# A decoder layer on one core: batches, placement and engines of the cross attention's work

## The chip, the cores and the metric

The kernel runs on one core of one Trainium2 chip. The time is the device time of one execution in microseconds (us). Below, "before" is the kernel as it stands, and the engines are TensorE (PE), its weight loads (PEld), VectorE (DVE), ScalarE (ACT), GpSimd (POOL) and SyncE's DMA queue (SP).

## What is computed

One pre-norm decoder layer on x of 2048 rows by 256, all in float32:

```python
x = x + attn(layernorm(x))          # 16 heads of 16, causal, ALiBi bias, softmax, Wo
x = x + xattn(layernorm(x), ctx)    # 16 heads of 64 over 1601 context rows
x = x + ffn(layernorm(x))           # fp8 x fp8 product with scales, bias in bf16

def xattn(query, ctx):              # q = query@Wq+bq, k = ctx@Wk+bk, v = ctx@Wv+bv
    scores = einsum('bqhd,bkhd->bhqk', q, k) / 8
    out = einsum('bhqk,bkhd->bqhd', softmax(scores), v).reshape(1, 2048, 1024)
    out = out @ Wo + bo + query
    return (out - mean(out)) * rsqrt(var(out) + 1e-5) * gamma + beta
```

The change touches the cross attention and the feed-forward part behind it; the self attention stays.

## The kernel before, in words

A Python class, `Order`, writes out by hand one list of stages; every engine's program walks this list in order and emits its own instructions for each stage, with waits on semaphores. So the list's order is each engine's order.

The cross attention goes over 8 head pairs (p = 0 to 7). Rows 0 to 63 of the array belong to a pair's first head, rows 64 to 127 to the second. Queries are cut into four blocks of 512 (b), keys into 13 tiles of 128 (j; the last has 65). A first sweep finds, for each query, the largest score: `pair_chunk` multiplies one tile of 128 queries with a quarter of the keys (400 columns, one bank for each head, L949), and VectorE reduces each bank to a maximum (L1257). There are 64 chunks a pair. `pair_rows` transposes a block's negated maxima on TensorE (L836), and SP's queue carries them into `shifts`. The second sweep makes, for each key tile, the scores of both heads in f32r (`pair_scores`, L964, three products high and low; the first two tiles also add the shifts, L972), ScalarE's exponentials (L1147), and the product with the values in plain f32 (`pair_values`, L984), which adds up in the bank `products`. The exponentials of the tiles are added up by GpSimd (L757, `add`); in pair 7, blocks 2 and 3, by VectorE. `pair_sums` multiplies that sum with ones (L996; in pair 7 the last three tiles go directly, L1002), `pair_invert` takes the inverses on VectorE (L1351), `pair_divide` multiplies (GpSimd L1509; in pair 7, blocks 2 and 3, VectorE L1356), `pair_project` multiplies with Wo (L1015), and VectorE adds the result to the residual (L1366).

There are 11 buffers of exponentials, two for each key tile, so 5.5 tiles. Four banks hold scores (two tiles); three banks go round among the chunks, projections, sums and transposes. Each f32 or f32r matmul leaves one or two records in the trace.

A batch is two key tiles: two stages of scores, then one run of values for the two tiles of the batch before. That makes seven runs for a block's 13 tiles. Everything else stands between these stages by `interleave` and `spread`: the maxima of blocks 2 and 3 of this pair and of blocks 0 and 1 of the next, and the next pair's projections of keys, queries (L782) and values (`value_tiles`, L937), each in a place of its own among the 80 places of a pair. The lags of sums, inverses, division and projection are counted in key tiles, passed in `pair_values`.

Pair 7 starts with `tail_weights`: VectorE quantises the feed-forward weights in one stage (L1220 to L1379). Behind each block's projection stands its `tail`: statistics, second norm, quantisation, transposition, product and store, spread by `TAIL_AT` over key tiles; most is VectorE's, with GpSimd's inverse roots (L1465, L1467).

## Time and profile before

| what | us |
|---|---|
| median of 3 runs | 1875.3 (1869.7 to 1883.9) |
| profiled execution | 1884.2 |
| its span | 1882.4 |
| TensorE busy | 1746.2 (93%) |
| VectorE busy | 1245.9 (66%) |
| GpSimd busy | 988.7 (53%) |
| ScalarE busy | 920.4 (49%) |

The self attention takes the first third of the span, up to about 610 us; the eight pairs of the cross attention follow from 643 us on. Busy times are sums of what the profiler recorded; a busy TensorE can still work below its peak, and the idle time of an engine that does not set the pace costs nothing.

### The profile page before, as it was taken

The page shows a single profiled execution, that of the slowest core. Times are in us where ns is not written, and L with a number is a line of the kernel's source. Part 1 is how long each engine was busy: PE and PEld are TensorE (multiplying, and loading weights), DVE is VectorE, ACT ScalarE, POOL GpSimd, SP SyncE. Part 2 cuts the span into 40 slices and gives each one's busy share as a digit, 9 for nine tenths or more (in the row PEclk, how much of TensorE's full clock was granted, in tenths as well). Part 3 has the DMA queues.
Part 4 walks back from the last instruction along what each step waited for, and adds up shares of the span by engine and source line. Part 5 has one row for each costly group of instructions (what it writes and reads, how often), then busy time and mean ns, then how long its engine had stood idle before and what let it go on. Part 6 is the DMA issues. An engine that isn't in the chain of part 4 may idle for free.

```text
span 1882.4 us, 29743 instructions
## 1 busy us (share of the span) xinstructions
PE 1746.2 (93%) x10698; PEld 886.5 (47%) x10698; DVE 1245.9 (66%) x2465; ACT 920.4 (49%) x1866; POOL 988.7 (53%) x840
## 2 busy tenths in 40 slices
PE   6989999999988999999999999999999999989973
PEld 3544434444444644555555555454555455444431
DVE  5777777778633565665675675666666566576888
ACT  2346666667665244345445444444544544544442
POOL 1000000000001386788898898898899799787311
PEclk9879999989988799999999999999999999989995
DMA  4332303331011000000000000000000000000001
GB/s 117 35 37 36 35 3 37 36 46 56 1 35 56 11 1 1 1 11 4 11 1 4 11 1 4 1 11 4 1 11 4 1 1 4 1 11 12 12 29 39
DMA packets 27947, 34.49 MB, mean 18 GB/s; under 512 B 4299, under 2 KB 25560, under 8 KB 26341
## 3 DMA queue, kind: packets, MB, share of 16 engines
q1 hardware_dynamic: 27354, 30.95, 9.1%
q8 instruction: 87, 1.43, 0.3%
q0 software_dynamic: 448, 1.64, 0.3%
q14 instruction: 58, 0.48, 0.1%
HBM read 14.99 MB, written 4.19 MB: 10 GB/s over the span
## 4 chain that ended last, share of the span: by engine, by line
PE 78%; DVE 16%; issue 3%; ACT 2%; POOL 1%; DMA 0%; ACTq 0%; SPq 0%; DVEq 0%; POOLq 0%
PE psum L984 18%; PE psum L964 14%; PE psum L949 9%; DVE maxima L1257 9%; PE psum L870 8%; PE psum L782 7%; PE psum L820 4%; PE psum L845 4%; PE psum L937 3%; PE psum L1015 3%; PE psum L882 2%; PE psum L996 2%; DVE parts_room L1351 1%; PE psum L897 1%; DVE stats L1204 1%
## 5 line engine op out<-in xcount | busy, mean ns | idle before, releaser
L1257 DVE TENSOR_REDUCE maxima<-psum 128x1 f32<-128x400 f32 (+5 forms) x1664 | 860.2, 580 | 312.0 <-PE psum L949 209.7
L757 POOL TENSOR_TENSOR parts_room<-parts_room,weights_room 128x512 f32<-128x512 f32 (+1 forms) x593 | 741.0, 1285 | 104.3 <-ACT weights_room L1147 104.2
L1147 ACT ACTIVATE weights_room<-psum 128x512 f32<-128x512 f32 (+1 forms) x757 | 406.5, 599 | 475.3 <-PE psum L964 404.9
L1075 ACT ACTIVATE weights_room<-psum 128x512 f32<-128x512 f32 (+3 forms) x640 | 300.1, 534 | 177.8 <-PE psum L845 98.7
L964 PE MATMUL psum<-stack_room,dk_hi 64*128 64x512 f32 (+1 forms) x1408 | 265.0, 410 | 6.5 <-ACT weights_room L1147 3.7
L949 PE MATMUL psum<-k_later,stack_room 64*128 64x400 f32 (+1 forms) x896 | 237.1, 404 | 12.6 <-DVE maxima L1257 11.4
L949 PEld LDWEIGHTS psum<-k_later,stack_room 64*128 64x128 f32 x896 | 128.9, 184 | 202.6 <-issue 124.9
L1471 POOL DMA_DIRECT2D parts_room<-ctx_dram x1 | 1.3, 1281 | 391.0 <-DMA stack_room<-alibi 391.0
L984 PE MATMUL psum<-weights_room,parts_room 128*64 128x512 f32 (+1 forms) x754 | 203.2, 606 | 0.0
L984 PE MATMUL psum<-weights_room,late_room 128*64 128x512 f32 (+1 forms) x760 | 202.3, 604 | 0.0
L845 PE MATMUL psum<-stack_room,stack_room 51*128 51x512 f32 (+3 forms) x640 | 141.0, 440 | 36.1 <-DVE maxima L1257 33.3
L870 PE MATMUL psum<-weights_room,v_self 128*32 128x512 f32 (+3 forms) x1280 | 170.5, 588 | 0.3 <-ACT weights_room L1075 0.3
L964 PE MATMUL psum<-stack_room,dk_lo 64*128 64x512 f32 (+1 forms) x704 | 165.8, 394 | 0.0
L964 PEld LDWEIGHTS psum<-stack_room,dk_hi 64*128 64x128 f32 (+1 forms) x1408 | 139.7, 182 | 43.9 <-issue 18.9
L1465 POOL TENSOR_SCALAR rstd<-meanvar 128x2 f32<-128x2 f32 (+1 forms) x24 | 9.6, 399 | 284.0 <-DVE meanvar L1207 284.0
L820 PE MATMUL psum<-stack_room,stack_room 51*128 51x512 f32 (+3 forms) x640 | 145.1, 457 | 6.0 <-DVE maxima L1257 5.5
L820 PEld LDWEIGHTS psum<-stack_room,stack_room 51*128 51x128 f32 x640 | 64.4, 198 | 130.5 <-issue 120.1
L1351 DVE RECIPROCAL parts_room<-parts_room 128x128 f32<-128x128 f32 x128 | 112.2, 920 | 9.2 <-ACT parts_room L1044 9.2
L845 PEld LDWEIGHTS psum<-stack_room,stack_room 51*128 51x128 f32 x640 | 67.1, 197 | 89.7 <-issue 75.8
L964 PEld LDWEIGHTS psum<-stack_room,dk_lo 64*128 64x128 f32 (+1 forms) x704 | 90.2, 182 | 11.5
L984 PEld LDWEIGHTS psum<-weights_room,late_room 128*64 128x64 f32 (+1 forms) x760 | 50.7, 136 | 83.2 <-issue 81.1
L984 PEld LDWEIGHTS psum<-weights_room,parts_room 128*64 128x64 f32 (+1 forms) x754 | 50.8, 136 | 82.3 <-issue 80.8
(138 smaller groups left out, 1912.3 us busy)
## 6 DMA issues: line engine op xcount, KB each, us to landing
stack_room<-parts_room SPq DMA_DIRECT2D x84, 128.0 KB
x_block<-x_dram SPq DMA_DIRECT2D x8, 512.0 KB, 4.9
x_middle<-x_block SPq DMA_DIRECT2D x4, 512.0 KB, 3.1
x_block<-x_middle SPq DMA_DIRECT2D x4, 512.0 KB, 3.8
out_dram<-x_block SPq DMA_DIRECT2D x8, 256.0 KB, 2.1
stack_room<-parts_room SPq DMA_DIRECT2D x24, 64.0 KB
parts_room<-ctx_dram POOLq DMA_DIRECT2D x1, 1536.0 KB, 7.9
stack_room<-shift_rows SPq DMA_DIRECT2D x64, 2.0 KB
```

The lines of the kernel that those rows point to most:

```text
L757: engine.tensor_tensor(sum_[:kw, :], old[:kw, :], weights[u % NP_WEIGHTS][:kw, :], ALU.add) \
L782: last = engine.matmul(slot[:, 0:n], lhs(kc), rhs(kc), start=kc == 0, stop=kc == DC - 1)
L820: last = engine.matmul(slots[m][:, 0:k1 - k0], q_stack[p % NSTACK][r, i * P:(i + 1) * P], k_stack[p % NSTACK][r, k0:k1], start=True, stop= ...
L845: last = engine.matmul(slots[m][:, 0:n], k_stack[p % NSTACK][r, j * P:(j + 1) * P], q_stack[p % NSTACK][r, q0:q0 + n], start=True, stop=j ...
L870: last = engine.matmul(products[c:c + COL, q0:BQ], v_self[:, j0 + n, h * VW:h * VW + COL], w_self[(s0 + n) % NW][:, m, 0:BQ - q0], start=j ...
L949: filled(use + n, engine.matmul(slot[:, 0:k1 - k0], q_hi[p % 2][r:r + DH2, i * P:(i + 1) * P], k_high(p)[r:r + DH2, k0:k1], start=True, st ...
L964: last = engine.matmul(pair_scores[u % NSCORES][:kw, :], k[r:r + DH2, at:at + kw], q[r:r + DH2, block(b)], start=first and n == 0, stop=no ...
L984: engine.matmul(products[r:r + DH2, :], v_pair[p % 2][:kw, j, r:r + DH2], weights[u % NP_WEIGHTS][:kw, :], start=j == 0, stop=j == NS - 1) \
L1075: engine.activation(w_self[s % NW][:, m, 0:n], bank_of(use + m)[:, 0:n], ACT.Exp, scale=SELF_SCALE).then_inc(emptied(use + m), 1)
L1147: engine.activation(weights[u % NP_WEIGHTS][:kw, :], pair_scores[u % NSCORES][:kw, :], ACT.Exp, scale=CROSS_SCALE).then_inc(pair_exp, 1)
L1257: engine.tensor_reduce(maxima[:, p % 2, i // TB, n, i % TB, ch:ch + 1], bank_of(use + n)[:, 0:real - k0], AX.X, ALU.max) \
L1351: engine.reciprocal(pair_recip[:, cols], pair_recip[:, cols]).then_inc(inverted, 1)
```

## The change

- A block's 13 tiles of scores go in batches of 3, 3, 3 and 4 (`BATCHES`), each followed by one run of values; all but the last run of a block leave their newest tile to the next run (`kept`).
- A second list, `chain`, counts in runs of values: sums follow one run after a block's end, the inverses one and two runs later, the division three, the projection four. In pair 7 the division comes after two runs and the projection after three; in its blocks 2 and 3 after one and two. `pass_step` now stands before each stage of scores.
- `beside` spreads the maxima evenly over the places of a pair except the last run of each block, and puts the next pair's projections directly ahead of given runs (`KEYS_AT`, `QUERIES_AT`, `TILES_AT`), with a keys' projection in the pair's first run. Value tiles of pair 0 stand ahead of the first scores.
- The keys get a third place, `k_spare`, in the room of the x blocks, for pairs 2, 4 and 6; GpSimd clears its last column. The loads of x for the last part wait until it is read.
- The loads of pair p + 2's weights move to the start of pair p.
- The quantisation of the feed-forward weights is cut into five pieces at runs 0, 3, 4 and 7 of pair 7 (`WEIGHTS_AT`).
- In pair 7, blocks 2 and 3, VectorE adds up only the first head's exponentials, GpSimd the second's; VectorE divides only block 3.
- In the tail the row scale is a stage of its own behind the transposition, the addition of beta moves from the statistics to the second norm, and the load of block b + 2 of x stands behind the store of block b; the first two loads stand at pair 7's start.

The diff, cut to its core (removed lines of `build` are left out):

```diff
-SUMS_LAG, PROJECT_LAG, LAST_PROJECT_LAG = 4, TB + 7, TB + 1
+PAIR_ROWS_LAG, FIRST_ROWS_LAG = 2, 1
+INVERT_AT, DIVIDE_AT, PROJECT_AT = (1, 1, 2, 2), 3, 4
+LAST_INVERT_AT, LAST_DIVIDE_AT, LAST_PROJECT_AT = (1, 1, 2, 2), 2, 3
+WEIGHTS_AT = (0, 0, 3, 3, 4, 7)
+BATCHES = (3, 3, 3, NS - 9)
+KEYS_AT, QUERIES_AT, TILES_AT = (0, 3, 3, 4), (7, 7, 8, 11), (11, 12, 15, 15)
+TAIL_AT, TAIL_APART = (1, 4, 7, 10, 13, 13, 15, 17), 3
...
+    def later(self, runs, what):
+        self.chain.append([runs, what])
+    def pass_run(self):
+        for item in list(self.chain):
+            item[0] -= 1
+            if item[0] <= 0:
+                self.chain.remove(item)
+                item[1]()
...
+    def pair_sweep1(self, p, b, lag):
+        steps = [(1, lambda i=i, ch=ch: self.put("pair_chunk", p, i, ch, banks=HP))
+                 for i in range(TB * b, TB * b + TB) for ch in range(len(CROSS_CHUNKS))]
+        steps.append((0, lambda: self.put("pair_negate", p, b)))
+        def rows():
+            self.put("pair_rows", p, b, banks=1)
+        return steps + [(0, (lambda: self.later(lag, rows)) if lag else rows)]
+    def pair_values(self, kept=0):
+        self.pass_run()
+        due, self.pending = self.pending[:len(self.pending) - kept], self.pending[len(self.pending) - kept:]
+        for p, b, j, s in due:
             self.put("pair_values", p, b, j, s)
             if j == NS - 1:
                 self.put("pair_finish", p, b)
                 if p < NP - 1:
-                    self.after(SUMS_LAG, lambda p=p, b=b: self.pair_sums(p, b))
+                    self.later(1, lambda p=p, b=b: self.pair_sums(p, b))
                 else:
                     self.pair_sums(p, b)
-        self.pending = []
     def pair_sums(self, p, b):
         self.put("pair_sums", p, b, banks=1)
-        at_once = 1 if p < NP - 1 else 2 if b < NB - 1 else TB
+        if p < NP - 1:
+            invert, divide, project = INVERT_AT, DIVIDE_AT, PROJECT_AT
+        elif b < NB // 2:
+            invert, divide, project = LAST_INVERT_AT, LAST_DIVIDE_AT, LAST_PROJECT_AT
+        else:
+            invert, divide, project = (1,) * TB, 1, 2
         for t in range(TB):
-            self.after(t // at_once + 1, lambda t=t: self.put("pair_invert", p, b, t))
-        self.after((TB - 1) // at_once + 1 + (at_once < TB), lambda: self.put("pair_divide", p, b))
-        lag = PROJECT_LAG if p < NP - 1 else LAST_PROJECT_LAG if b < NB - 1 else 2
-        self.after(lag, lambda: self.pair_out(p, b))
+            self.later(invert[t], lambda t=t: self.put("pair_invert", p, b, t))
+        self.later(divide, lambda: self.put("pair_divide", p, b))
+        self.later(project, lambda: self.pair_out(p, b))
...
     def pair_sweep2(self, p):
-        batch = []
         def scores(b, j):
+            self.pass_step()
             self.put("pair_scores", p, b, j, self.step)
-            batch.append((p, b, j, self.step))
+            self.pending.append((p, b, j, self.step))
             self.step += 1
-        def values():
-            self.pair_values()
-            self.pending, batch[:] = list(batch), []
         steps = []
         for b in range(NB):
-            for j0 in range(0, NS, 2):
-                steps += [(1, lambda b=b, j=j: scores(b, j), b) for j in range(j0, min(NS, j0 + 2))]
-                steps.append((min(NS, j0 + 2) - j0, values, b))
+            j0 = 0
+            for n in BATCHES:
+                steps += [("scores", lambda b=b, j=j: scores(b, j)) for j in range(j0, j0 + n)]
+                j0 += n
+                steps.append(("values", lambda kept=int(j0 < NS): self.pair_values(kept)))
         return steps
...
     def tail(self, b):
-        self.put("tail_load", b)
         banks = {"turn": 1, "product": 1}
-        for n, kind in enumerate(("statistics", "add_norm", "to_fp8", "rounded", "turn", "product", "store")):
+        def store(i):
+            self.put("tail_store", b, i)
+            if i and b + 2 < NB:
+                self.put("tail_load", b + 2)
+        for n, kind in enumerate(("statistics", "add_norm", "to_fp8", "rounded", "turn", "row_scale", "product")):
             for i in range(2):
                 self.after(TAIL_AT[n] + TAIL_APART * i,
                            lambda kind=kind, i=i: self.put("tail_" + kind, b, i, banks=banks.get(kind, 0)))
+        for i in range(2):
+            self.after(TAIL_AT[-1] + TAIL_APART * i, lambda i=i: store(i))
...
+    def key_block(self, p, b):
+        self.put("project_keys", p, b, banks=1)
+        self.put("key_steps", p, b)
+        if b:
+            self.put("key_rests", p, b - 1)
+    def query_block(self, p, b):
+        self.put("project_queries", p, b, banks=1)
+        if b == 0:
+            self.put("key_rests", p, NK - 1)
+    def tile_block(self, p, n):
+        self.put("value_tiles", p, n, banks=1)
...
+    def beside(self, main, maxima, others):
+        runs = [n for n, (kind, _) in enumerate(main) if kind == "values"]
+        places = [n for n in range(len(main)) if n not in runs[len(BATCHES) - 1::len(BATCHES)]]
+        ahead = [[] for _ in main]
+        for block, steps in enumerate(maxima):
+            groups = []
+            for work, step in steps:
+                if work:
+                    groups.append([])
+                groups[-1].append(step)
+            here = places[len(places) * block // len(maxima):len(places) * (block + 1) // len(maxima)]
+            for n, group in enumerate(groups):
+                ahead[here[n * len(here) // len(groups)]] += group
+        for n, step in others:
+            ahead[runs[n]].append(step)
+        for (_, step), side in zip(main, ahead):
+            for what in side + [step]:
+                what()
...
+        now(self.pair_queries(0) + self.pair_sweep1(0, 0, 0))
+        def block(make, p, n):
+            return lambda: make(p, n)
+        for n in range(len(VALUE_TILES)):
+            self.tile_block(0, n)
         for p in range(NP):
+            maxima = [self.pair_sweep1(p, b, FIRST_ROWS_LAG if (p, b) == (0, 1) else PAIR_ROWS_LAG)
+                      for b in range(NB // 2 if p else 1, NB)]
+            if p < NP - 1:
+                maxima += [self.pair_sweep1(p + 1, b, PAIR_ROWS_LAG) for b in range(NB // 2)]
+                others = [(at, block(make, p + 1, n)) for make, all_at in
+                          ((self.key_block, KEYS_AT), (self.query_block, QUERIES_AT), (self.tile_block, TILES_AT))
+                          for n, at in enumerate(all_at)]
             else:
+                put("tail_weights_load")
+                put("tail_load", 0), put("tail_load", 1)
+                maxima += [[], []]
+                others = [(at, lambda n=n: put("tail_weights", n)) for n, at in enumerate(WEIGHTS_AT)]
+            if p + 2 < NP:
+                put("pair_load", p + 2)
+            self.beside(self.pair_sweep2(p), maxima, others)
+        while self.chain or self.soon:
+            self.pass_run()
+            self.pass_step()
...
-    def on_vector(p, b):
-        return p == NP - 1 and b >= NB // 2
+    def divided_on_vector(p, b):
+        return p == NP - 1 and b == NB - 1
+    def summed_on_vector(p, b, m):
+        return p == NP - 1 and b >= NB // 2 and m == 0
...
-        return k_later if p else k_first
+        return k_later if p % 2 else k_spare if p else k_first
...
-                    if p >= 2:
-                        act.wait_ge(*bank_filled(use_of["pair_chunk", p - 1, NT - 1, len(CROSS_CHUNKS) - 1] + HP - 1))
+                    if p == 2:
+                        act.wait_ge(normed, 2 * NB)
+                        for i in range(2):
+                            act.wait_ge(middle_out[i], 32)
+                    elif p > 2:
+                        act.wait_ge(*bank_filled(use_of["pair_chunk", p - 2, NT - 1, len(CROSS_CHUNKS) - 1] + HP - 1))
...
-                engine.tensor_tensor(out_scale, scales[:, 0:1], scales[:, 1:2], ALU.mult) \
-                    .then_inc(dve_step, 1)
-                chain.count += 1
-                engine.reciprocal(inv_scales, scales).then_inc(inverse_made, 1)
-                dve.wait_ge(w8_scaled, 1)
+                n, = at
                 flat = w8.rearrange("p c n -> p (c n)")
-                chain.on(quantise(0, flat))
-                after_last()
-                not_a_number_past_448(quant_m[0], flat, quant_m[0])
-                engine.tensor_tensor(flat, flat, quant_m[0], ALU.add).then_inc(w8_made, 1)
+                if n == 0:
+                    dve.wait_ge(tails_in, 16 * 6)
+                    chain.on(engine.tensor_tensor(out_scale, scales[:, 0:1], scales[:, 1:2], ALU.mult))
+                    engine.reciprocal(inv_scales, scales).then_inc(inverse_made, 1)
+                elif n == 2:
+                    dve.wait_ge(w8_scaled, 1)
+                    chain.on(round_unit(0))
+                elif n == 3:
+                    round_up(0)
+                elif n == 4:
+                    chain.on(round_down(0, flat))
+                elif n == 5:
+                    after_last()
+                    not_a_number_past_448(quant_m[0], flat, quant_m[0])
+                    engine.tensor_tensor(flat, flat, quant_m[0], ALU.add).then_inc(w8_made, 1)
             elif kind == "tail_statistics":
                 b, i = at
                 dve.wait_ge(*bank_read(use_of["pair_project", NP - 1, b] + i))
...
+                sp.wait_ge(*bank_filled(use_of["pair_chunk", NP - 2, NT - 1, len(CROSS_CHUNKS) - 1] + HP - 1))
```

## Rows read from the trace of the kernel before

**Rows 1.** The page: the chain that ended last, shares of the span by engine.

```profile
PE 78%; DVE 16%; issue 3%; ACT 2%; POOL 1%; DMA 0%; ACTq 0%; SPq 0%; DVEq 0%; POOLq 0%
```

**Rows 2.** Stretches: us, length, busy us (records) of PE, PEld, DVE, ACT, POOL, then clock, DMA.

```profile
646.75:812.22 165.47, 156.25 (x847) 81.38 (x848) 103.84 (x198) 67.75 (x131) 122.89 (x101) 0.99 0.02 7
812.22:956.32 144.10, 143.54 (x802) 74.51 (x802) 90.92 (x169) 68.86 (x133) 126.56 (x104) 1.00 0.02 5
...
1676.84:1718.02 41.18, 34.23 (x183) 17.80 (x182) 28.31 (x47) 15.10 (x29) 28.32 (x23) 0.88 0.00 1
1718.02:1755.12 37.10, 34.86 (x199) 17.81 (x197) 27.24 (x54) 15.09 (x29) 26.32 (x23) 1.00 0.05 15
1755.12:1790.98 35.86, 33.00 (x178) 15.30 (x177) 31.20 (x70) 18.12 (x37) 5.82 (x9) 0.95 0.07 23
1790.98:1840.90 49.92, 39.49 (x196) 17.17 (x194) 44.01 (x101) 19.07 (x38) 8.74 (x13) 0.93 0.10 31
1840.90:1882.40 41.50, 9.49 (x40) 5.56 (x40) 34.16 (x83) 8.55 (x17) 5.60 (x8) 0.56 0.10 34
```

**Rows 3.** TensorE in time order: start us, duration us, line, output<-inputs, shape, records.

```profile
1125.94 1.94 PE L984 MATMUL psum<-weights_room,late_room 128*64 128x512 f32 x8
1127.80 0.45 PE L949 MATMUL psum<-k_later,stack_room 64*128 64x400 f32 x2
1128.09 0.63 PE L964 MATMUL psum<-stack_room,dk_hi 64*128 64x512 f32 x4
...
1128.79 0.90 PE L949 MATMUL psum<-k_later,stack_room 64*128 64x400 f32 x2
...
1130.59 0.64 PE L984 MATMUL psum<-weights_room,late_room 128*64 128x512 f32 x1
```

**Rows 4.** TensorE in time order: projections and value tiles between f32r work, pairs 2 and 3.

```profile
1041.41 1.98 PE L782 MATMUL psum<-norm_room,parts_room 128*128 128x512 f32 x4
1043.23 1.89 PE L1015 MATMUL psum<-parts_room,parts_room 128*128 128x256 f32 x8
...
1122.88 2.05 PE L937 MATMUL psum<-parts_room,parts_room 128*128 128x128 f32 x16
1124.87 0.73 PE L964 MATMUL psum<-stack_room,dk_hi 64*128 64x512 f32 x4
```

**Rows 5.** All engines in time order, in brackets idle time and its releaser; one batch.

```profile
1002.87 0.18 PEld L949 LDWEIGHTS psum<-k_later,stack_room 64*128 64x128 f32 x2 [0.81 <-issue]
...
1003.35 2.98 DVE L1257 TENSOR_REDUCE maxima<-psum 128x1 f32<-128x400 f32 x6 [1.55 <-PE psum L949]
...
1003.98 0.18 PEld L949 LDWEIGHTS psum<-k_later,stack_room 64*128 64x128 f32 x1 [0.17 <-DVE maxima L1257]
...
1004.05 2.06 ACT L1147 ACTIVATE weights_room<-psum 128x512 f32<-128x512 f32 x4 [5.71 <-PE psum L964]
...
1004.94 0.18 PEld L949 LDWEIGHTS psum<-k_later,stack_room 64*128 64x128 f32 x1 [0.21 <-DVE maxima L1257]
1005.42 0.20 PEld L996 LDWEIGHTS psum<-parts_room,ones_v 128*64 128x64 f32 x4 [0.30 <-DVE maxima L1257]
```

**Rows 6.** GpSimd's additions: count, shortest, median and longest ns of one.

```profile
L757 POOL TENSOR_TENSOR parts_room<-parts_room,weights_room x593: 1255/1283/1705, 656.1 to 1748.9; 128x512 f32<-128x512 f32 x177, 65x512 f32<-65x512 f32 x21
```

**Rows 7.** GpSimd, VectorE, TensorE around pair 7's start; the VectorE line later, alone.

```profile
1678.44 3.10 POOL L757 TENSOR_TENSOR parts_room<-parts_room,weights_room 65x512 f32<-65x512 f32 x2
...
1678.80 1.63 DVE L1224 TENSOR_TENSOR parts_room<-parts_room 128x512 f32<-128x512 f32 x1
...
1685.01 0.70 PE L949 MATMUL psum<-k_later,stack_room 64*128 64x400 f32 x1 [6.91 <-DVE maxima L1257]
...
1807.33 0.69 DVE L1224 TENSOR_TENSOR parts_room<-parts_room 128x512 f32<-128x512 f32 x1
```

**Rows 8.** VectorE's additions after 1738 us (count, busy us, mean ns); TensorE's wait.

```profile
L757 DVE TENSOR_TENSOR parts_room<-parts_room,weights_room 128x512 f32<-128x512 f32 x30 | 18.7, 681 | 0.0
...
1835.54 1.56 PE L996 MATMUL psum<-parts_room,ones_v 128*64 128x512 f32 x4 [4.14 <-DVE parts_room L757]
```

96 lines of the change are left out of this document (34 added, 62 removed).

## The prediction

> **What bounds the kernel now.** I read the views in this order. The chain of waits [rows 1] gives TensorE 78% of the span, VectorE 16%, GpSimd 1%. The stretches [rows 2] say where: I cut them at the first score matmul of head pair 0 (646.75 us), of pair 1 (812.22), of pair 7 (1676.84), at each query block of pair 7, and at the end of its last sums (1840.90). Everything before 646.75 us is untouched except 16 matmuls of value tiles. Pairs 1 to 6, from 812.22 to 1676.84, are one period six times: 864.6 us, 144.1 each; in pair 1, which stands for them, TensorE is busy 143.54 of 144.10, GpSimd 126.56, VectorE 90.92, ScalarE 68.86. So TensorE's queue sets the pace there, GpSimd is 12% behind it. In pair 7 VectorE takes over: busy 31.20 of 35.86 us in block 2 and 44.01 of 49.92 in block 3, and after 1840.90 the last block's chain runs almost alone for 41.50 us.
>
> A busy TensorE is not one at its peak, so I went into the matmuls of one period [rows 3]. Times here are differences of start times. A run of values over two key tiles lasts from 1125.94 to 1127.80: 1.86 us, that is 0.86 a tile (two records of each head side by side, 0.43 a step) and 0.14 on top. Then the kind of matmul changes from f32 to f32r: the first chunk of the maxima costs 0.29 before the score matmul starts, where an undisturbed one costs 0.18. A key tile of scores costs 0.70 (1128.09 to 1128.79), with four products, as for the first two tiles of a block, 0.93. Going back to f32 costs another 0.1. One run of values between f32r work therefore costs about 0.14 + 0.1 + 0.1 = 0.34 us beyond its work. An f32 projection that stands alone before a score tile pays the same; the value-tile block at 1122.88 [rows 4] is one.
>
> The second loss is VectorE's turn on the three banks. In [rows 5] the second matmul of the second chunk loads its weights at 1003.98, 1.11 us after the first chunk at 1002.87, held by VectorE; the next such wait ends at 1004.94, and VectorE needs 2.98 us for six reductions, 0.50 each. The f32 run behind can start 0.48 us after that last load (1005.42). So a burst of chunks is a VectorE-paced chain: the n-th bank is free 1.11 + 0.5 x (n-1) us after the burst began.
>
> **The change, part by part.**
>
> *Batches.* Per query block 7 runs of values become 4 (batches of 3, 3, 3, 4 key tiles; one tile is kept back, so the runs hold 2, 3, 3, 5 tiles). 12 runs fewer per pair x 0.34 = 4.1 us. The 12 projection blocks per pair, of which about 8 stand before a score tile rather than before a run (13 of 20 places of a block are score tiles), now all stand at a run: 8 x 0.3 = 2.4 us. Together 6.5 us.
>
> But the burst gets longer: 4 chunks and 3 tiles. In [rows 3] a batch of two takes 2.79 us from 1127.80 to 1130.59 (the burst of [rows 5] 2.55). For a batch of three, the eighth matmul of chunks waits for the fifth reduction, 1.11 + 4 x 0.5 = 3.11 us; plus 0.48 is 3.58 us. TensorE alone would need 0.29 + 3 x 0.70 + 3 x 0.18 + 0.1 = 3.0, so 0.5 to 0.6 is VectorE's. The batch of four has no chunk before its run: last chunk at about 3.25, then 0.18 + 0.70 + 0.1, so 4.2 us. Block: 3 x 3.58 + 4.2 = 14.9, values 13 x 0.86 + 4 x 0.14 = 11.7, sum 26.7; four blocks 106.7. Around them, as before: sums 4 x 0.91, output projections 4 x 1.83, value tiles 3 x 1.89 + 0.6, keys 3 x 1.72 + 0.3, queries 4 x 1.72 (four f32 matmuls at 0.43), four transposes: 30.4 ([rows 4] show three of these kinds: a query block of four matmuls, 1.82 us to the next start, value tiles, 1.99 with the switch, and an output projection, 1.89 us to the end of its last record; without the switch I take 0.43 a matmul). About 0.1 us at each of some dozen runs for a bank not yet read: 1. **New period 138 us, 6 less**; six pairs: 37.
>
> Does GpSimd let it? Its 96 additions at 1.25 us back to back (mean record 1.283, [rows 6]), four divisions and four key rests make 129 to 132 us a pair. That fits under 138 with 6 to 9 us to spare, a third of today's slack (17.5). Within a block the additions of a batch take 7.5 us where a batch with its run lasts 6.3, so GpSimd falls behind by 1.2 us in each of two batches and catches up in the runs that carry projections. The 11 weight buffers are 5.5 tiles deep; that lag is under two tiles. Division now stands in GpSimd's queue behind the four tiles of the last batch, and the projection that needs it comes one run later, about 1 to 2 us after it. Tight, but free in my sum; without the cover it costs its lateness, up to 1 us a block, 4 a pair.
>
> ScalarE: four exponentials in 2.06 us [rows 5], 1.03 a tile, against 0.88 for scores and a chunk on TensorE. With four score banks the fourth tile of a batch waits 0.1 to 0.2 us; inside the rounding.
>
> The keys of the next pair now come in the first run, for which a third key buffer lies in the x rooms; the old order had them later. Their copies precede VectorE's split, and the next batch's first reduction can come 0.7 us late, once a pair. The loads of weights move to the pair's start on SP's queue; their readers are a pair away.
>
> *Pair 0.* 165.47 us from 646.75. Now 80 chunks lie evenly over 64 places, so a batch of three carries five: 1.11 + 6 x 0.5 + 0.48 = 4.6 us, the last batch about 5. Block 18.8 + 11.7 = 30.5, four 122; projections, fewer sums 26; one row of maxima asked for at once, 1.5: 149.5. Value tiles run ahead of everything, 9 us from 643.2 at the half clock that the stretch starts with. Ends at 802 instead of 812: **10 less** (range 3 to 18).
>
> *Pair 7, first half.* The quantisation of the weights stood as one piece at its head: VectorE's chain kept TensorE idle for 6.91 us [rows 7], and the granted clock over that block was 0.88 [rows 2], score matmuls at half speed until about 1697, some 4 us. In five pieces at four runs it needs at most 3.7 us of VectorE during 4.4 us of values, so nothing shows. Blocks 0 and 1: 2 x (26.7 + 0.2) + three projections 5.5 + sums 0.9 + two direct sums 7.3 = 67.5 against 41.18 + 37.10 = 78.3: 11 less (of which 3.6 of sums moved out of block 2).
>
> *Pair 7, second half.* Bound by VectorE: additions of blocks 2 and 3, 36 at 0.68 [rows 8], one head's half moves to GpSimd: 18 x 0.68 = 12.3 off, and one division. What comes back: in [rows 7] the add of two SBUF tensors at 1678.80, beside GpSimd additions, took 1.63 us; the same line at 1807.33, alone, 0.69. So each addition on VectorE beside one on GpSimd costs up to 0.94 more: 18 x 0.94 = 17 at worst, 0 at best; nearer 10, since VectorE is often elsewhere when GpSimd adds. TensorE without chunks runs ahead of ScalarE: batches of three cost 2.9, of four 4.0 us; with sums and projection 32 to 33 us a block, under today's 35.86. The 4.14 us wait for the last additions [rows 8] shrinks. I take 77 us for blocks 2 and 3 (65 by TensorE alone; 84 if every addition collides, 77 + 7) against 85.8. The end chain loses 3: the last x block is loaded only when block 1's store is out, and more of block 2's tail is left for it: 44.5 against 41.5. Pair 7: 67.5 + 77 + 44.5 = 189 against 205.6: **17 less** (range 0 to 28).
>
> The Trainium skill bears on this step: "SBUF — State Buffer", section "Who interferes with whom", says that a VectorE instruction with two SBUF inputs contends with a GpSimd instruction that reads SBUF, while one from PSUM does not. The trace agrees where it can be seen (1.63 against 0.69 us). By that rule at full strength the moved half wins nothing, 17 back for 12.3 off, and pair 7 would end 7 us later than in my sum.
>
> **Sum.** 37 + 10 + 17 = 64 us. The profiled execution took 1884.2 us (span 1882.4 and 1.8 around it), so 1820 on its own scale; it lies 9 above the median of the three runs, 1875.3, which I predict for: **1811 us**.
>
> **Rivals.**
> 1. *The burst eats the saving.* If VectorE's chain in a batch of three lasts 4.1 instead of 3.58 us (chunks that also wait behind reciprocals and key splits), the 12 batches give back 6 us and pairs 1 to 6 stay at 144. For it: VectorE already ends many TensorE waits. Against: reductions sit at 0.50 us each and VectorE has 53 us free a pair. Only pairs 0 and 7 gain: 1875 - 27 = 1848. Chance 0.09.
> 2. *It goes better.* TensorE's waits for banks partly vanish and GpSimd's 131 us becomes the period: 13 less a pair, 78, plus 27: 1770. Chance 0.11.
> 3. *Every addition on VectorE collides with one on GpSimd*: 17 us back instead of 10, and if half of the 32 two-input tail steps of blocks 0 to 2 beside them collide too, 16 x 0.5 = 8 more: 1818 to 1826, within my range. Chance 0.2 of the forecast's 0.72, with its time inside that range.
> 4. *Slower: GpSimd becomes the bound.* The same queue holds additions, division and key rests, and the projection at the first run of each block waits for it. An addition records 1.283 us in the mean but up to 1.705 [rows 6]. Above 1.41 us, 96 of them with 8 us of the rest pass today's 144.1; TensorE then idles at each block's first run and may drop to the lower of its two clocks. The point from which it decides is 1.46 us, where six pairs lose the 27 that pairs 0 and 7 gain. At 1.55: 157 a pair, 13 x 6 = 78 lost, 27 gained, 1926. Against: 1.25 back to back today, and in pairs 1 to 6 the VectorE work beside it stays the same. Chance 0.04.
> 5. *No change.* Batches alone matter little and division or a late load costs what they save: 1870. Chance 0.04.
>
> **How the numbers follow.** Forecast with rival 3: 0.72. Its own range: pairs 1 to 6 gain 20 to 60, pair 0 3 to 18, pair 7 0 to 28: summed 1769 to 1852, about 1782 to 1843 when not all ends meet. For 8 in 10 I go a little into rivals 1 and 2: 1778 to 1848. A difference under 1% (1857 to 1894) is about what can't be told from no change. Faster 0.92 (forecast 0.72, rivals 1 and 2), within 1% 0.04 (rival 5), slower 0.04 (rival 4).
>
> **What the profile after would show.** Steps right: 16 runs of values a pair, a period near 138 us with TensorE still over 99% busy and GpSimd near 93%; three-tile bursts of 3.5 to 3.6 us; no 6.91 us hole at pair 7. Wrong: bursts of 4 us or more (rival 1); TensorE waiting for the division or for the last addition at the first run of a block, additions above 1.4 us (rival 4); additions of pair 7 on VectorE above 1.2 us (rival 3); a VectorE wait for the last x block over 5 us.

## The result, and the profile after

The changed kernel takes 1855.06 us (median of 4 runs, 1851.39 to 1858.07), the kernel before 1874.76 on the same chip: a ratio of 0.987, 95% interval 0.983 to 0.992. It is faster by 1.3%, which the interval keeps clear of no change, but by 20 us and not by the 64 that were forecast; the forecast of 1811 us and its range up to 1848 missed. The profiled execution took 1858.07 us, its span is 1855.9.

The page's first lines show the shift. The columns of the second are busy us, share of the span and instructions; the last is the chain that ended last.

```profile
span 1855.9 us, 29773 instructions
PE 1699.3 (92%) x10698; PEld 892.9 (48%) x10698; DVE 1255.6 (68%) x2446; ACT 910.4 (49%) x1866; POOL 1012.0 (55%) x860
...
PE 55%; issue 21%; DVE 16%; POOL 6%; ACT 1%; DMA 1%; POOLq 0%; ACTq 0%; DVEq 0%
```

GpSimd has 6% of the chain where it had 1% [rows 1]. The stretches, cut as in [rows 2] but at the first shift matmul of a block: pair 0, pair 1, blocks 0 to 2 of pair 7, block 3, and what follows its last sums. The columns are those of [rows 2].

```profile
651.70:801.32 149.62, 144.87 (x813) 78.25 (x811) 99.62 (x193) 67.48 (x132) 124.20 (x102) 1.00 0.02 7
801.32:940.83 139.51, 137.08 (x804) 75.59 (x800) 91.07 (x171) 67.41 (x133) 124.64 (x104) 1.00 0.02 5
1638.48:1678.45 39.97, 35.59 (x197) 17.74 (x195) 30.54 (x45) 15.85 (x31) 27.16 (x22) 0.91 0.00 1
1678.45:1714.23 35.78, 34.11 (x199) 18.31 (x197) 31.45 (x66) 14.89 (x29) 28.00 (x25) 1.00 0.00 1
1714.23:1759.00 44.77, 35.45 (x178) 15.58 (x176) 36.65 (x63) 18.35 (x37) 19.84 (x18) 0.89 0.02 6
1759.00:1808.50 49.50, 35.06 (x164) 16.36 (x162) 41.50 (x78) 17.83 (x35) 20.27 (x20) 0.86 0.07 22
1808.50:1855.90 47.40, 11.29 (x49) 5.91 (x45) 35.20 (x85) 8.98 (x18) 5.01 (x8) 0.59 0.12 39
```

Pair 0 fell from 165 to 149.6 us, the forecast's 149.5. Pairs 1 to 6 fell from 144.1 to 139.5 each (forecast 138). Pair 7, cut in the same way in both traces, rose from 204.9 to 217.4 us, where 189 had been forecast. That is the miss: 28 of the 38 us between the forecast's 1820 on the profiled execution's scale and its 1858.

Two things stand out in pair 7. VectorE was given 18 additions and one division fewer in blocks 2, 3 and the end, yet it is busy 36.65 + 41.50 + 35.20 = 113.35 us there; the same cut before shows 108.60 (the first line):

```profile
1755.92:1882.40 126.48, 81.19 (x405) 37.35 (x401) 108.60 (x249) 45.74 (x91) 20.07 (x29) 0.82 0.09 30
```

And the head, where [rows 7] had a stall of 6.91 us, now has one of 3.46, from a product of two numbers. These lines are VectorE, GpSimd and TensorE in order of time:

```profile
1642.12 4.91 DVE L1443 TENSOR_TENSOR norm_room<-norm_room 128x1 f32<-128x1 f32 x1
1646.95 0.15 DVE L1444 RECIPROCAL norm_room<-norm_room 128x2 f32<-128x2 f32 x1
...
1642.07 2.50 POOL L812 TENSOR_TENSOR parts_room<-weights_room,weights_room 128x512 f32<-128x512 f32 x2
1644.52 2.50 POOL L812 TENSOR_TENSOR parts_room<-parts_room,weights_room 128x512 f32<-128x512 f32 x2
...
1647.75 1.97 PE L1053 MATMUL psum<-parts_room,ones_v 128*64 128x512 f32 x4 [3.46 <-DVE stack_room L1436]
```

VectorE's multiplication of one element per partition begins beside four GpSimd additions and ends when they do. The 0.15 us reciprocal behind it shows what so small an instruction costs undisturbed.

### The profile page after: what moved, and what is told of

It is laid out like the page before. It is cut to its first block, busy times and chain, and to the rows that moved or that the text cites. A ratio compares the mean times of both kernels' runs of the same rounds, so it can differ in the third digit from the quotient of the medians.

```text
span 1855.9 us, 29773 instructions
## 1 busy us (share of the span) xinstructions
PE 1699.3 (92%) x10698; PEld 892.9 (48%) x10698; DVE 1255.6 (68%) x2446; ACT 910.4 (49%) x1866; POOL 1012.0 (55%) x860
## 4 chain that ended last, share of the span: by engine, by line
PE 55%; issue 21%; DVE 16%; POOL 6%; ACT 1%; DMA 1%; POOLq 0%; ACTq 0%; DVEq 0%
PE psum L1041 11%; DVE maxima L1327 9%; PE psum L1021 8%; PE psum L925 8%; PE psum L1006 5%; POOL parts_room L812 4%; PE psum L875 4%; PE psum L837 4%; PE psum L900 4%; PE psum L992 2%; PE psum L937 2%; PE psum L1072 1%; PE psum L1053 1%; POOL parts_room L1592 1%; PE psum L952 1%
## 5 line engine op out<-in xcount | busy, mean ns | idle before, releaser
L812 POOL TENSOR_TENSOR parts_room<-parts_room,weights_room 128x512 f32<-128x512 f32 (+1 forms) x607 | 759.7, 1295 | 95.7 <-ACT weights_room L1208 94.7
L1208 ACT ACTIVATE weights_room<-psum 128x512 f32<-128x512 f32 (+1 forms) x757 | 394.8, 608 | 284.4 <-PE psum L1021 251.1
L1021 PE MATMUL psum<-stack_room,dk_hi 64*128 64x512 f32 (+1 forms) x1408 | 288.9, 411 | 5.9 <-ACT weights_room L1208 5.9
L1041 PE MATMUL psum<-weights_room,parts_room 128*64 128x512 f32 (+1 forms) x754 | 191.8, 598 | 0.0
L1021 PE MATMUL psum<-stack_room,dk_lo 64*128 64x512 f32 (+1 forms) x704 | 188.4, 391 | 0.0
L900 PE MATMUL psum<-stack_room,stack_room 51*128 51x512 f32 (+3 forms) x640 | 139.6, 436 | 36.3 <-DVE maxima L1327 34.7
L1021 PEld LDWEIGHTS psum<-stack_room,dk_hi 64*128 64x128 f32 (+1 forms) x1408 | 151.7, 180 | 23.7 <-ACT weights_room L1208 9.6
L1006 PE MATMUL psum<-k_later,stack_room 64*128 64x400 f32 (+1 forms) x512 | 137.9, 392 | 2.1 <-DVE maxima L1327 1.7
L1006 PEld LDWEIGHTS psum<-k_later,stack_room 64*128 64x128 f32 x512 | 81.1, 184 | 89.8 <-issue 51.1
L1021 PEld LDWEIGHTS psum<-stack_room,dk_lo 64*128 64x128 f32 (+1 forms) x704 | 107.0, 180 | 10.6 <-issue 0.2
L1006 PE MATMUL psum<-x_room,stack_room 64*128 64x400 f32 (+1 forms) x384 | 101.1, 391 | 0.0
```

Of the source, the lines that this page charges most:

```text
L812: engine.tensor_tensor(sum_[:kw, :], old[:kw, :], weights[u % NP_WEIGHTS][:kw, :], ALU.add) \
L900: last = engine.matmul(slots[m][:, 0:n], k_stack[p % NSTACK][r, j * P:(j + 1) * P], q_stack[p % NSTACK][r, q0:q0 + n], start=True, stop=j ...
L1006: filled(use + n, engine.matmul(slot[:, 0:k1 - k0], q_hi[p % 2][r:r + DH2, i * P:(i + 1) * P], k_high(p)[r:r + DH2, k0:k1], start=True, st ...
L1021: last = engine.matmul(pair_scores[u % NSCORES][:kw, :], k[r:r + DH2, at:at + kw], q[r:r + DH2, block(b)], start=first and n == 0, stop=no ...
L1041: engine.matmul(products[r:r + DH2, :], v_pair[p % 2][:kw, j, r:r + DH2], weights[u % NP_WEIGHTS][:kw, :], start=j == 0, stop=j == NS - 1) \
L1208: engine.activation(weights[u % NP_WEIGHTS][:kw, :], pair_scores[u % NSCORES][:kw, :], ACT.Exp, scale=CROSS_SCALE).then_inc(pair_exp, 1)
```

## The experiments

Three theories for pair 7. **A**: VectorE's instructions with SBUF operands are held by GpSimd's additions, so moving one head's additions to GpSimd gives back what it saves. **B**: the order: batches of three, and sums, projections and tail steps placed in coarse runs, make one engine's queue stand still for another. **C**: the single instruction at the head. The table holds the us from one block's first shift matmul to the next one's, each from its own trace; "period" is one of pairs 1 to 6, which repeat within 0.1 us in every trace but for pair 1 in e8_tail2_5 (0.8 shorter) and e12_batches2 (0.3 shorter). The ratio is to the kernel before, of several runs, with its interval; it is too wide to rank kernels a few us apart, so the readings go by the traces. Each kernel has one trace, and pair 7 varies by some 3 us for nothing but the granted clock (below, 193.1 against 195.8 and 195.9 us), so a difference of that size in pair 7 shows nothing by itself.

| kernel | period | pair 7, blocks 0, 1, 2, 3 with the end | pair 7 | ratio |
|---|---|---|---|---|
| before | 144.1 | 41.2, 37.2, 35.8, 90.6 | 204.9 | 1 |
| changed | 139.5 | 40.0, 35.8, 44.8, 96.9 | 217.4 | 0.987 (0.983 to 0.992) |
| e1_old_pair7 | 139.5 | 48.1, 36.3, 34.5, 93.7 | 212.6 | 0.978 (0.972 to 0.985) |
| e2_vector_adds | 139.5 | 39.9, 35.8, 41.0, 93.3 | 210.0 | 0.979 (0.974 to 0.984) |
| e3_pool_adds | 139.5 | 37.2, 35.8, 39.4, 98.6 | 211.1 | 0.981 (0.976 to 0.987) |
| e4_outscale | 139.5 | 33.7, 35.8, 46.0, 97.9 | 213.4 | 0.985 (0.978 to 0.993) |
| e13_base (e2 and e4) | 139.5 | 33.7, 35.8, 42.0, 93.7 | 205.3 | 0.978 (0.973 to 0.983) |
| e5_tail2_3 | 139.5 | 33.7, 35.8, 40.7, 91.0 | 201.3 | one run |
| e8_tail2_5 | 139.5 | 33.7, 35.8, 41.4, 88.8 | 199.7 | one run |
| e9_sums_lag | 139.5 | 30.2, 36.2, 32.7, 100.6 | 199.8 | one run |
| e7_early_out | 138.5 | 33.4, 53.7, 40.9, 83.4 | 211.3 | one run |
| e6_half_old | 139.5 | 33.7, 35.8, 33.3, 90.4 | 193.1 | 0.974 (0.971 to 0.977) |
| e10_half_old_split | 139.5 | 33.7, 35.8, 37.0, 94.8 | 201.4 | 0.980 (0.975 to 0.986) |
| e11_half_old_proj5 | 138.5 | 33.4, 36.5, 31.8, 94.0 | 195.8 | 0.969 (0.966 to 0.973) |
| e15_best2 | 138.5 | 33.4, 35.8, 33.1, 93.6 | 195.9 | 0.972 (0.968 to 0.976) |
| e12_batches2 | 144.6 | 37.8, 41.1, 36.1, 98.5 | 213.6 | 0.998 (0.995 to 1.002) |
| e14_half_maxima | 138.7 | 33.7, 34.8, 42.3, 93.9 | 204.7 | one run |

**Pair 7 in the order before** (methods of the kernel before called for p == NP - 1, additions and divisions of its blocks 2 and 3 on VectorE, the weights' six pieces put one behind the other at its head).

> Pairs 0 to 6 as in the changed kernel, pair 7 in the order of the kernel before: batches of two key tiles, sums and tail counted in key tiles, all additions and divisions of blocks 2 and 3 on VectorE, the weights quantised in one go at the head. In the changed kernel pair 7 took 217.4 us from its first score matmul to the end (204.9 before) where 189 had been forecast. If pair 7's own new order costs that, this kernel's pair 7 takes 205 again and the whole about 1842 us, ratio to the kernel before 0.981 to 0.983. If instead pair 7 is slow because of what pairs 0 to 6 leave behind (GpSimd further back, a lower granted clock, x rooms taken by the third key buffer), it stays at 215 or more and the ratio at 0.987 to 0.989.

Measured 212.6 us for pair 7, neither 205 nor 217. Blocks 2 and 3 with the end got 13.5 us shorter, so their new order and the split of the additions, both undone here, cost. But block 0 got 8 longer, and theory C's instruction points to the reason: here it took 8.54 us, beside a row of nine GpSimd instructions, from the third on (the last four lines).

```profile
1621.52 8.54 DVE L1495 TENSOR_TENSOR norm_room<-norm_room 128x1 f32<-128x1 f32 x1
...
1618.95 6.18 POOL L864 TENSOR_TENSOR parts_room<-parts_room,weights_room 128x512 f32<-128x512 f32 x5
1625.10 1.27 POOL L864 TENSOR_TENSOR parts_room<-parts_room,parts_room 128x512 f32<-128x512 f32 x1
1626.33 2.49 POOL L864 TENSOR_TENSOR parts_room<-parts_room,weights_room 65x512 f32<-65x512 f32 x2
1628.78 1.25 POOL L1644 TENSOR_TENSOR parts_room<-parts_room,parts_room 128x512 f32<-128x512 f32 x1
```

In the kernel before, the same product got its turn as one addition gave way to the next (VectorE, then GpSimd):

```profile
1675.30 0.55 DVE L1370 TENSOR_TENSOR norm_room<-norm_room 128x1 f32<-128x1 f32 x1
...
1672.05 3.78 POOL L757 TENSOR_TENSOR parts_room<-parts_room,weights_room 128x512 f32<-128x512 f32 x3
1675.74 1.32 POOL L757 TENSOR_TENSOR parts_room<-parts_room,parts_room 128x512 f32<-128x512 f32 x1
```

So what pairs 0 to 6 leave in GpSimd's queue decides whether such an instruction takes half a microsecond or eight. In this one way the second reading of the expectation, that pair 7 is slow by what pairs 0 to 6 leave behind, is true.

**Additions of pair 7's blocks 2 and 3.** All on VectorE:

```diff
     def divided_on_vector(p, b):
-        return p == NP - 1 and b == NB - 1
+        return p == NP - 1 and b >= NB // 2
     def summed_on_vector(p, b, m):
-        return p == NP - 1 and b >= NB // 2 and m == 0
+        return p == NP - 1 and b >= NB // 2
```

> One part undone: all 36 additions and the divisions of pair 7's blocks 2 and 3 on VectorE, none on GpSimd; batches and places stay. Theory A (VectorE instructions with two SBUF inputs are held up by GpSimd additions beside them): the steps of the tail fall back to their undisturbed lengths, and blocks 2, 3 and the end (141.7 us from the first score of block 2) get 5 to 9 us shorter although VectorE has 18 more additions. Theory B (what costs is where the coarse runs put sums, projections and tail steps in the queues): VectorE gets 18 x 0.68 = 12 us more to do and the stretch gets 5 to 12 us longer.

And all on GpSimd (`return False` in summed_on_vector):

> The other direction: all 36 additions of pair 7's blocks 2 and 3 on GpSimd, none on VectorE. Theory A: VectorE loses 14.2 us of additions, but GpSimd is busy twice as long beside its tail; those that stay collide more; net 0 to 6 us shorter over the 141.7 us from block 2 on, and VectorE's tail steps get longer in the mean. Theory B: VectorE is not what ends the waits, the stretch stays within 2 us. If the last additions of a block now come later on GpSimd than on VectorE (1.25 to 1.43 us each against 0.68), the sums wait for them and it gets longer.

Theory A. From block 2 on the changed kernel takes 141.7 us; with all on VectorE 134.3, 7.4 less, and VectorE's busy time falls from 113.35 to 107.32 us although it has 18 additions and a division more. With all on GpSimd it is 138.0 (3.7 less, not far above the spread named above), and VectorE is busy 114.1 us with no addition left. So all on VectorE beats the split clearly, all on GpSimd by little. The tail's steps tell where it goes: VectorE's groups from block 2 on, in the changed kernel (count, busy us, mean ns of one, idle before):

```profile
L812 DVE TENSOR_TENSOR parts_room<-parts_room,weights_room 128x512 f32<-128x512 f32 x16 | 12.6, 788 | 0.9
L1487 DVE TENSOR_SCALAR norm_room<-x_room,meanvar,rstd 128x256 bf16<-128x256 f32 x16 | 10.6, 706 | 0.0
...
L1291 DVE TENSOR_TENSOR norm_room<-parts_room 128x512 bf16<-128x512 f32 x8 | 8.4, 1051 | 0.3
...
L1283 DVE TENSOR_SCALAR parts_room<-parts_room 128x512 f32<-128x512 f32 x8 | 6.3, 784 | 0.3
...
L1500 DVE TENSOR_REDUCE norm_room<-norm_room 128x2 f32<-128x512 bf16 x8 | 5.4, 671 | 0.0
```

and the same lines with all additions on VectorE:

```profile
L812 DVE TENSOR_TENSOR parts_room<-parts_room,weights_room 128x512 f32<-128x512 f32 x30 | 19.8, 716 | 0.0
...
L1487 DVE TENSOR_SCALAR norm_room<-x_room,meanvar,rstd 128x256 bf16<-128x256 f32 x16 | 5.7, 402 | 0.0
...
L1291 DVE TENSOR_TENSOR norm_room<-parts_room 128x512 bf16<-128x512 f32 x8 | 5.5, 692 | 0.3
...
L1500 DVE TENSOR_REDUCE norm_room<-norm_room 128x2 f32<-128x512 bf16 x8 | 5.4, 672 | 0.0
L1283 DVE TENSOR_SCALAR parts_room<-parts_room 128x512 f32<-128x512 f32 x8 | 3.4, 427 | 0.3
```

The additions themselves lengthened little (788 ns against 716 here and 681 in [rows 8]); what grew are some of the tail's tensor_scalar and tensor_tensor instructions, by up to 0.36 us each in the mean, while the reduction (L1500) did not move. Added up over all of VectorE's instructions, 18 additions at 0.68 us (12.3) went and the busy time still rose by 6.0, so about 18 us came back. GpSimd pays too: its additions there take 1432 ns where the median was 1283 [rows 6].

**The product of scales.**

```diff
-  chain.on(engine.tensor_tensor(out_scale, scales[:, 0:1], scales[:, 1:2], ALU.mult))
+  chain.on(engine.tensor_scalar(out_scale, scales[:, 0:1], scales[:, 1:2], None, ALU.mult))
```

> The 128x1 product of two scales at the head of pair 7, which took 4.91 us beside two GpSimd additions (0.55 in the kernel before), is written as a tensor_scalar with the second scale as its per-partition scalar: one SBUF tensor as input instead of two. Theory C (two tensors from SBUF are what is held up): it takes under 0.6 us, the 3.46 us wait of TensorE at the second batch of block 0 goes, block 0 of pair 7 falls from 40.0 to 36 us, and the whole by 4 us (ratio 0.985). Rival: any small VectorE instruction from SBUF to SBUF is held there, or TensorE's low clock is not from this wait; nothing moves.

Theory C. The instruction begins beside the same GpSimd additions and is over in 0.20 us; block 0 falls from 40.0 to 33.7 us, 6.3 against the 4 expected, since the low clock behind the stall goes too (granted 0.91 over the block before, 1.00 now). The kernel with all additions on GpSimd keeps the two apart: it has the stall (product 4.87 us, wait 3.47), but a granted clock of 1.00, and its block 0 takes 37.2 us. So 3.5 us are the wait and 2.8 the clock. Pair 7 as a whole falls by 4.0 us only, since blocks 2 and 3 with the end take 143.9 us here against 141.7.

```profile
1650.97 0.20 DVE L1443 TENSOR_SCALAR norm_room<-norm_room 128x1 f32<-128x1 f32 x1
...
1649.66 1.25 POOL L1592 TENSOR_TENSOR parts_room<-parts_room,parts_room 128x512 f32<-128x512 f32 x1
1650.88 2.49 POOL L812 TENSOR_TENSOR parts_room<-weights_room,weights_room 128x512 f32<-128x512 f32 x2
```

Not every VectorE instruction from SBUF to SBUF is held, then; this one with a single tensor operand of one element is not. A later one with one operand is: the weights' 128x512 int32 tensor_scalar (L1281) took 3.88 us in this trace (0.42 in the median of its nine), unnoticed by TensorE: block 1 takes 35.8 us as in the other traces.

**Both edits.**

> The changed kernel with two edits only: additions and divisions of pair 7's blocks 2 and 3 on VectorE, and the product of scales as a tensor_scalar. If the two effects (7.4 and 6.3 us, the second with up to 2.3 us given back later) add up, pair 7 takes 203.7 us and the whole about 1842, ratio 0.982. If they overlap (the trace with only the product changed gave back 2.3 us in blocks 2 and 3) it is 206 us and 0.983. If they help each other, under 201.

205.3 us: 12.1 of the 13.7 add up. This is the base of the next readings; the texts below took it as 203.7, which is 1.6 too low.

**The tail of block 2 later**, by three and by five key tiles (`+ 3 * (b == NB - 2)` on its places in `tail`); in the second, KEYS_AT begins with 1 as well.

> Base of this and the next three: all additions and divisions of pair 7's blocks 2 and 3 on VectorE, and the product of scales as a tensor_scalar. From the two traces its pair 7 should be 33.6 + 35.8 + 41.0 + 93.3 = 203.7 us (block 3 with the end being the last). Edit: the tail of block 2 is moved three key tiles later in the queues. Theory B (ScalarE's queue stands at a tail step of block 2 that waits 10.6 us for VectorE, the last exponentials of block 3 are behind it, TensorE waits 8.8 us): that wait falls under 3 us, VectorE's idle 6.9 us before the last inverses is filled, block 3 with the end falls from 93.3 by 4 to 8 us. Rival: VectorE's work is the bound wherever it stands (107 us busy of 134); then what is moved comes back in the end chain, and the sum stays within 2 us.

> Two edits in stretches that do not touch. Pair 7: the base, and the tail of block 2 five key tiles later instead of three. Theory B: the ScalarE wait ahead of the last exponentials is gone altogether, but both last tails now stand one behind the other at the end; against three tiles later within 3 us. If VectorE is the bound wherever its work stands, block 3 with the end stays 93.3. Pairs 1 to 6: the first block of keys is projected at the second run instead of the first. The 0.91 and 0.32 us waits behind VectorE's split at the first run go; the period falls by up to 1.2 us, or by nothing if the split then holds the second run as long.

Theory B, in part. Block 3 with the end takes 91.0 and 88.8 us against 93.7 in the base, pair 7 4.0 and 5.6 less. In the changed kernel ScalarE stood at a tail step with the last exponentials behind it:

```profile
1801.18 0.72 ACT L1235 ACTIVATE parts_room<-norm_room,norm_room 128x512 f32<-128x512 bf16 x1 [11.22 <-DVE norm_room L1487]
1801.81 1.06 ACT L1208 ACTIVATE weights_room<-psum 65x512 f32<-65x512 f32 x2
...
1802.44 2.45 PE L1041 MATMUL psum<-weights_room,late_room 65*64 65x512 f32 x4 [7.16 <-ACT weights_room L1208]
```

That wait of TensorE (9.9 us in the base) is gone in both, but most of its price comes back: with three tiles it waits 13.9 us for last additions (7.0 in the base), with five 25.3 us for the last tails' roundings (16.7). VectorE is busy 107 of 132 and of 130 us from block 2 on, and taking a wait of 9.9 us away shortened block 3 with the end by 2.7 and 4.9. The keys' part won nothing: block 0 of a pair got 0.7 us longer, block 1 0.7 shorter.

**The sums of a block two score tiles later.**

```diff
                 if p < NP - 1:
                     self.later(1, lambda p=p, b=b: self.pair_sums(p, b))
+                elif b < NB - 1:
+                    self.after(3, lambda p=p, b=b: self.pair_sums(p, b))
                 else:
```

> Base as before (additions and divisions of blocks 2 and 3 on VectorE, product of scales as a tensor_scalar; by the runs so far 33.7 + 35.8 + 41 + 93.3 = 203.8 us for pair 7). One edit: the sums of pair 7's blocks 0 to 2 are put two score tiles into the next block instead of right behind the block's last values, which is where the order before had them. Theory B1 (what block 2 loses is that its sums stand right behind its last values, so TensorE waits 5.9 to 7.0 us for VectorE's last additions with nothing else in its queue): block 2 and 3 together fall from 134.3 by 4 to 7 us. Theory B2 (it is the batches of three and the tail steps, not this place): within 2 us of 134.3.

199.8 us against 205.3: 5.5 less, which speaks for theory B1, by one trace on each side (the cut between blocks moves with the sums, so pair 7's total counts). In the base, behind the end of block 2, TensorE had nothing but the sums in its queue and waited 7.0 us for VectorE's last additions, which stood behind 8 us of the tail. The order before had two score tiles in between.

**Projections of blocks 0 and 1 earlier in pair 7, output projections later in pairs 0 to 6** (LAST_INVERT_AT, LAST_DIVIDE_AT, LAST_PROJECT_AT = (1, 1, 1, 1), 1, 2; PROJECT_AT = 5 instead of 4).

> Two edits in stretches that do not touch. Pair 7: the base, and sums, inverses, division and projection of blocks 0 and 1 one run earlier, so their tails start three key tiles earlier. Theory B: block 2 falls from 41.0 by 3 to 6 us, as less of the tails of blocks 0 and 1 stands in it; if places do not matter it stays. Pairs 0 to 6: the output projection one run later, so that it never waits for GpSimd's division (0.65 us at the first run of each block). If that wait costs what it shows, the period falls from 139.5 to 137 us; if the time is TensorE's own or comes back as a wait for an addition, it stays.

Two readings. The earlier tails cost 18 us in block 1 (53.7 against 35.8) and won 10 at the end, but only 1.2 in block 2 where 3 to 6 were expected: tail steps now stand between the reductions of block 1's maxima, and TensorE waits for those, 9.0 us in all and 5.46 the longest. The first half of pair 7 has no room for tails. In pairs 1 to 6 the later projection took 1.0 us off the period; pair 0 got 0.5 longer. The expectation had laid 0.65 us to each block; the changed kernel's trace shows a wait of 0.65 for the division once a pair, so 2.5 us was too much.

**Blocks 2 and 3 in the order before, blocks 0 and 1 in the new one**, with the base's two edits (old_sweep2 and what it calls are the methods of the kernel before).

```diff
+            sweep = self.pair_sweep2(p)
+            if p < NP - 1:
+                self.beside(sweep, maxima, others)
+            else:
+                self.beside(sweep[:len(sweep) // 2], maxima[:2], others)
+                for _, step, b in self.old_sweep2(p):
+                    if b >= NB // 2:
+                        step()
```

> Blocks 0 and 1 of pair 7 in the changed kernel's order with the weights in pieces, blocks 2 and 3 in the order of the kernel before (batches of two, tail counted in key tiles passed by the runs of values), all their additions on VectorE, the product of scales as a tensor_scalar. Theory B (the batches of three and the coarse places cost in blocks 2 and 3): block 2 takes 34.5 and block 3 with the end 93.7 us as in the run with the whole of pair 7 in the old order, pair 7 33.6 + 35.8 + 128.2 = 197.6 us, the whole about 1835 (ratio 0.978). Rival (the old order was quicker there only because its longer head had given VectorE and GpSimd time to catch up): 134 us as in the run with all additions on VectorE, pair 7 203.7.

193.1 us, 12.2 under the base and 11.8 under the kernel before. That is 4.5 better than expected, since blocks 2 and 3 take 123.7 us where e1 had 128.2; no run tells why. Then one head's additions to GpSimd again:

> The kernel with pair 7's blocks 2 and 3 in the order before (33.3 + 90.4 = 123.7 us there, pair 7 193.1, ratio 0.974), with one edit: the additions of head 1 in these blocks on GpSimd, as in the changed kernel. Theory A: VectorE has 18 additions fewer, 12 us, but its other steps with SBUF operands are held by them; VectorE's busy time stays at 108 us or rises, and the two blocks take 123.7 to 132 us (they lose 7.4 us in the other order). If the split saves what was forecast, VectorE's busy time falls to 98 to 102 us and the blocks take about 116 to 120 us.

8.3 us worse, and VectorE's busy time from block 2 on rises from 108.02 to 112.61 us with 18 instructions fewer, so about 17 us came back for 12.3. Theory A holds in either order, with the same size (7.4 and 8.3). Which instructions pay depends on what stands beside them: here the additions themselves do (first line; 680 ns with all on VectorE), and the tail's tensor_scalar, which took 706 ns in the changed kernel, does not (second).

```profile
L866 DVE TENSOR_TENSOR parts_room<-parts_room,weights_room 128x512 f32<-128x512 f32 x16 | 13.9, 869 | 0.8
...
L1541 DVE TENSOR_SCALAR norm_room<-x_room,meanvar,rstd 128x256 bf16<-128x256 f32 x16 | 5.7, 399 | 0.0
```

The busy times by stretch:

```profile
1700.50:1824.10 123.60, 78.64 (x385) 35.60 (x381) 108.02 (x247) 44.72 (x89) 22.33 (x27) 0.79 0.08 26
...
1704.80:1836.90 132.10, 82.38 (x387) 37.61 (x383) 112.61 (x229) 44.59 (x90) 44.98 (x45) 0.77 0.07 24
```

The first line is of the kernel with all on VectorE, the second of the split one.

**What helped, together.**

> The two parts that helped together: pair 7's blocks 2 and 3 in the order before, and the output projection of pairs 0 to 6 one run later. If they add up, period 138.5 instead of 139.5 in pairs 1 to 6 and pair 7 at 193 us: 6 us under the former kernel's, ratio 0.971 (about 1821 us where the kernel before takes 1875). If the later projection of pair 6's last block pushes work into pair 7's head, pair 7 grows by 1 to 3 us.

> As the kernel with pair 7's blocks 2 and 3 in the order before and the output projection of pairs 0 to 6 one run later, but pair 6's last block projected at its former run. If that block alone had lengthened pair 7 (195.8 instead of 193.1 us), pair 7 is back at 193 and the period stays 138.5: 2.7 us less, ratio 0.968. If not, 195.8 stays and the difference comes from where the engines stand when pair 7 begins.

The period is 138.5 in both, and the better of the two measurements is 1821.65 us, beside 1878.59 of the kernel before on the same chip: ratio 0.969, against 0.987 of the changed kernel. Pair 7 takes 195.8 and 195.9 us where the kernel with the earlier projection took 193.1, so pair 6's last block is not the cause. The instructions are the same and so is the wait of TensorE for ScalarE at block 3's second score tile (2.86 and 3.02 us), but the 14.3 us behind block 3's first score ran at a granted clock of 0.88 in the kernel with the earlier projection and of 0.64 (of the two levels 1.2 and 2.4 GHz mostly the lower) in the last one, and fewer instructions fit into them. Why the clock stayed low for longer is not shown.

```profile
1733.70:1748.00 14.30, 11.44 (x58) 5.04 (x56) 11.07 (x27) 9.45 (x20) 3.43 (x2) 0.88 0.05 18
...
1727.70:1742.00 14.30, 11.28 (x36) 3.95 (x32) 8.92 (x23) 6.76 (x14) 3.42 (x2) 0.64 0.05 18
```

**Batches of two everywhere** (BATCHES = (2,) * 6 + (NS - 12,), the places in runs scaled).

> The changed kernel with batches of two key tiles (seven runs of values a block) in all pairs; the places given in runs are scaled so that each part comes about where it was, projections still stand at runs. Forecast's account (each run of values between f32r work costs 0.34 us beyond its work, 12 more a pair): the period of pairs 1 to 6 rises from 139.5 to 143.6 us. If what was won came from putting the projections at the runs, or from the later division, it stays at 139.5 to 141. If batches were worth more (longer bursts hide VectorE's pace), it goes over 145.

The period is 144.6 us, so the batches of three are worth 5.1, and the rest of the new order in pairs 1 to 6 nothing: with batches of two it stands 0.5 above the kernel before. This trace has no wait for the division, as the kernels with the later projection have none; against their 138.5 the batches are worth 6.1. Pair 0 keeps its gain without them and is even 2.0 us shorter (147.6), so its gain comes from the even spread of the maxima or from the value tiles ahead of it; no run takes these two apart.

**Half of each reduction left out** (the maxima over half of the keys).

> As e13, but the reductions of the maxima in the cross attention read only the first half of each bank's columns (the maxima of half of the keys; this part of the computation is left out). Forecast's account: a burst of three tiles and four chunks is paced by VectorE (3.41 us measured, 3.0 by TensorE's matmuls alone), so with a reduction of about 0.3 us instead of 0.5 each of the 12 such bursts of a pair gets 0.3 to 0.5 us shorter and the batch of four 0.2; the period falls from 139.5 by 4 to 6 us. Rival: bursts are set by TensorE or ScalarE (four score banks, 1.03 us a tile for the exponentials) and the period stays within 1 us; or GpSimd (124.6 us busy) becomes the next limit and the saving stops near 2 to 3 us.

A reduction takes 0.36 us instead of 0.50, VectorE's busy time in a period falls from 91 to 68 us, and the period from 139.5 to 138.7. The waits for VectorE before the chunks' weight loads (7.4 us a period) vanish, yet a burst of three still takes 3.38 us (3.41 before). These are its four chunks and the run behind it, tiles left out:

```profile
1007.41 0.45 PE L1006 MATMUL psum<-k_later,stack_room 64*128 64x400 f32 x2
...
1008.39 0.36 PE L1006 MATMUL psum<-k_later,stack_room 64*128 64x400 f32 x2
...
1009.27 0.37 PE L1006 MATMUL psum<-k_later,stack_room 64*128 64x400 f32 x2
...
1010.30 0.56 PE L1006 MATMUL psum<-k_later,stack_room 64*128 64x402 f32 x2
1010.79 2.80 PE L1041 MATMUL psum<-weights_room,parts_room 128*64 128x512 f32 x12
```

A chunk with its tile takes 0.98, 0.88 and 1.03 us, and from the last chunk to the f32 run it is 0.49 us where the forecast's sum had 0.28 (0.18 and 0.1 for the switch). In pairs 1 to 6 VectorE hardly paces the bursts. In pair 0, with five chunks to a batch, it does: 142.5 against 149.6 us.

## Why the prediction was right or wrong, step by step

- **Pair 0** (149.5 us, 10 less): right, 149.6, and pair 1 begins 11.6 us earlier. Of these, 1.8 belong to the code ahead, whose last transposition starts that much earlier in this trace (641.28 against 643.04), so 9.8 are pair 0's. VectorE's chain as its pace is borne out by the halved reductions.
- **Batches** (12 runs fewer x 0.34 = 4.1 us a pair): right in kind, 5.1 measured, 6.1 with the division out of the way. The switch back to f32 was underpriced (0.3 instead of 0.1, by the halved reductions), the burst overpriced (3.58 against 3.41 us, the batch of four 4.2 against 4.15).
- **Projections at the runs** (8 x 0.3 = 2.4 us): wrong. With batches of two and projections at the runs the period is 0.5 us above the kernel before, and there it held no wait for the division. This term and the division (1.0) were too favourable by more than the 1.5 us a period that were missing, 9 us in six pairs; the batches, worth more than forecast, hid the rest.
- **VectorE's part in a burst** (0.5 to 0.6 us of each): wrong in cause. The waits read from [rows 5] were real, but taking them away gives 0.8 us a period, not 12 x 0.5. A wait that ends just as another limit is reached has no price. What holds the third tile for 0.15 us was not settled.
- **Division "tight, but free", up to 4 a pair if not**: it cost 1.0. The keys in the first run (0.7 us late): a wait of 0.91 is there, but moving it won nothing.
- **GpSimd 129 to 132 us, fits**: it fits, at 124.6 us of 139.5 (89% where 93% stood; TensorE is busy 98.3% where over 99% stood). Rival 4 did not occur.
- **Pair 7, first half** (67.5 us; "in five pieces nothing shows"): 75.8 measured. The failing term is the product of scales, costed at nothing in "at most 3.7 us of VectorE": it took 4.91 by itself. Neither its two operands in SBUF nor GpSimd beside them were counted, though [rows 7] had a two-operand instruction at 1.63 for 0.69 us beside GpSimd. Written as a tensor_scalar, blocks 0 and 1 take 33.7 + 35.8 = 69.5.
- **Pair 7, second half** (12.3 us off VectorE, 10 back, one division more off; 77 + 44.5): 141.7 measured against 121.5. The sign of the split was wrong: it costs 7.4 to 8.3 us. The term "18 x 0.94 = 17 at worst" was taken at 10; about 18 and 17 us came back, so its worst case was the case, though by another road: it priced the additions alone, and in the changed kernel they grew by only 0.1 us each, while the tail's instructions, an add-on in rival 3, carried most of the loss. The forecast cited the Trainium skill, "SBUF — State Buffer", section "Who interferes with whom", and by that rule at full strength put pair 7 at 7 us more. The trace agrees in the direction and in the size of what comes back, but 7 us are a third of the 20 by which the second half missed. The same section also says that tensor_scalar can enter a mode that contends with GpSimd, and that reductions never do. The trace agrees: 427 to 784 ns for L1283, a tensor_scalar, and 672 and 671 for L1500, a reduction.
- **What the forecast did not have at all**: the order of blocks 2 and 3. "With sums and projection 32 to 33 us a block" took TensorE's work as if no queue stood in between. Blocks 2 and 3 in the order before give back 12.2 us (the base against e6). Sums right behind a block's last values are 5.5 of them, by one trace; the rest lies in the batches of three and the places of the tail steps, and how it divides is open.
- **The sum.** 217.4 - 12.1 (collisions at head and additions) - 12.2 (order of blocks 2 and 3) = 193.1, against 189 forecast. Of the 4.1 us left, 2.0 stand in blocks 0 and 1 and 2.1 behind them, and the granted clock alone moves pair 7 by 2.8; the 189 also held a gain of 2.3 by the split, which does not exist. That the sum comes this close once the split and the new order are undone is in part luck.

## What to carry to other kernels

Before work is moved from VectorE to GpSimd to share a load, look at everything that VectorE reads and writes in SBUF meanwhile, instructions with two SBUF tensors first, then tensor_scalars on large tiles: it is they that can pay, however small, and a tiny one that must wait for GpSimd's next pause can hold the whole chain behind it. When a queue's order is made coarser, look at each point where an engine has only one thing left to do (here the sums behind a block's last values), and keep two tiles of other work there. A wait in the trace is worth only what the next limit leaves; a run with the suspected work cut down prices it.

## What the runs showed of the hardware that had not been expected

- A VectorE instruction with two SBUF operands was held not for one GpSimd instruction but through a whole row of them: 4.91 us beside four additions (4.85 and 4.87 in two more traces), 8.54 us beside a row of nine, from the third on, and in the two traces shown until GpSimd's row ended. It is not always so: 0.55 us in the kernel before, beside a row that went on. "Who interferes with whom" of the Trainium skill's "SBUF — State Buffer" speaks of a block for the whole instruction; here it outlasted several.
- Sharing has its price on both sides: GpSimd's additions take 1.43 us in the mean beside VectorE's tail, where the median in the kernel before was 1.28 [rows 6].
- The stretch ahead of the first shift matmul, the same code in all the changed kernels, took from 635.45 to 660.54 us from trace to trace, with a mean granted clock of 0.95 and 0.90, while a period of pairs 1 to 6 repeated within 0.1 us at a clock of 1.00. TensorE is busy 88 to 90% of the first and 98% of the second. So a good part of the spread between executions is likely to arise ahead of the cross attention; the lines are those of e11 and e4:

```profile
0.00:635.45 635.45, 561.27 (x4314) 278.56 (x4316) 433.92 (x907) 362.44 (x787) 28.93 (x43) 0.95 0.24 39
...
0.00:660.54 660.54, 593.34 (x4314) 292.57 (x4316) 434.60 (x907) 362.50 (x787) 28.93 (x43) 0.90 0.23 38
```
